# A four-layer graph network on one core: the source node numbers of all edges stay in SBUF, and the product tile of the third edge phase is held in quads

## The reference, cut to what matters

```python
sa  = ex / denom[edge_dst]                                    # layer 0: 4 heads of 16, scores q[src] * k[dst]
agg = segment_sum(sa[:, :, None] * v[edge_src], edge_dst)
h_edge = ((atom[src] + bond) @ W).reshape(-1, H, D)           # layer 1: 2 heads of 64, softmax over dst
se  = concatenate([h[src], eh]); att = sum(q * (se @ W_k))    # layer 2: 1 head of 64, softmax over dst
h   = relu(combined @ msg_w1[l] + msg_b1[l])                  # layer 3: combined = [x[src], edge features]
x   = _layernorm(x + layer(x, src, dst, ...))                 # after every layer
```

## Time and profile before

| | |
|---|---|
| median of 3 runs | 14026.2 us (14020.19 to 14042.77) |
| the profiled execution, its own time | 14023.7 us |
| its span, first to last instruction | 14022.0 us |
| PE busy | 2267.2 us (16%) |
| DVE busy | 4894.6 us (35%) |
| ACT busy | 3146.0 us (22%) |
| POOL busy | 6487.0 us (46%) |
| mean granted TensorE clock | 0.575 of full speed |
| DMA traffic | 1046.03 MB, mean 75 GB/s; 239 GB/s in the first fortieth of the span, 34 to 90 after it |

### The profile page before, as it was taken

The page is one execution under the profiler, slowest core; times in us unless marked ns, Lnnn a source line. Parts: engine busy times, 40 slices in busy tenths (PEclk is TensorE's granted clock), DMA queues, the critical chain, the costliest instruction groups (busy, mean ns, idle before and its releaser), DMA issues. The chain is left out here.

```text
span 14022.0 us, 92846 instructions
## 1 busy us (share of the span) xinstructions
PE 2267.2 (16%) x11897; PEld 1811.0 (13%) x11897; DVE 4894.6 (35%) x6191; ACT 3146.0 (22%) x3841; POOL 6487.0 (46%) x6837
## 2 busy tenths in 40 slices
PE   2000000002000000000344433444432111111112
PEld 1000000001000000000244333433330000000002
DVE  3443333345444444445222222222242222222223
ACT  0221111114111111112132222332232222222222
POOL 6644444456544444444544444444434444444444
PEclk6555555555555555555677777777765555555556
DMA  6222222221222222222222222222212222222222
GB/s 239 81 73 70 74 70 74 70 90 34 63 66 65 65 70 68 65 65 81 61 79 78 71 77 80 79 79 71 77 44 68 70 67 72 72 72 72 71 71 69
DMA packets 418910, 1046.03 MB, mean 75 GB/s; under 512 B 198760, under 2 KB 226218, under 8 KB 403804
## 3 DMA queue, kind: packets, MB, share of 16 engines
q1 hardware_dynamic: 177424, 680.51, 13.0%
q0 software_dynamic: 219488, 334.23, 10.0%
q10 hardware_dynamic: 21612, 27.96, 0.6%
HBM read 633.14 MB, written 401.95 MB: 74 GB/s over the span
## 5 line engine op out<-in xcount | busy, mean ns | idle before, releaser
L982 POOL DMA_INDIRECT se<-x_table,edge_ix x1481 | 1400.8, 946 | 1855.7 <-DMA edge_ix<-in_src 815.7
L982 POOL DMA_INDIRECT hidden<-hidden_table,edge_ix x1468 | 1388.7, 946 | 1761.0 <-DMA edge_ix<-in_src 1289.8
L982 POOL DMA_INDIRECT g<-x_table,edge_ix x1468 | 1388.5, 946 | 1648.8 <-DMA edge_ix<-in_src 1169.1
L982 POOL DMA_INDIRECT qv<-qv_table,edge_ix x1443 | 1378.6, 955 | 1404.4 <-DMA edge_ix<-in_src 865.8
L1144 ACT ACTIVATE edge_sums<-edge_val 128x1904 f32<-128x1904 f32 (+3 forms) x220 | 1116.4, 5075 | 1084.9 <-issue 1050.9
L1837 DVE TENSOR_TENSOR edge_product<-mk_ps,edge_q_now 128x256 f32<-128x256 f32 x391 | 166.1, 425 | 2308.8 <-ACT edge_msg L1772 2262.0
L1134 DVE TENSOR_TENSOR_SCAN edge_val<-edge_bank,edge_val 128x464 f32<-128x464 f32 (+1 forms) x715 | 687.6, 1032 | 672.0 <-ACT edge_val L1940 441.6
L1932 PE MATMUL edge_e_ps<-w_nodes,edge_ea_t 128*128 128x512 f32 x784 | 476.6, 774 | 2733.9 <-DMA edge_ea_t<-in_edge_attr 1165.2
L1982 DVE TENSOR_TENSOR hidden<-hidden,edge_e_ps 128x3584 f32<-128x3584 f32 x55 | 213.8, 3888 | 1799.2 <-DMA hidden<-edge_sync_rows 1232.4
L1727 PE MATMUL mk_ps<-w_mk,edge_se_t 128*128 128x128 f32 x3128 | 523.1, 320 | 1656.6 <-issue 1399.5
L1087 ACT ACTIVATE edge_bank<-edge_weight_arg 128x112 f32<-128x112 f32 (+2 forms) x171 | 38.9, 228 | 2939.9 <-issue 1980.9
(11 more groups left out here) (463 smaller groups left out, 8657.6 us busy)
## 6 DMA issues: line engine op xcount, KB each, us to landing
edge_sync_rows<-x_table SPq DMA_DIRECT2D x6656, 0.2 KB
sums<-edge_sums SPq DMA_DIRECT2D x55, 1848.0 KB
sums<-edge_sums SPq DMA_DIRECT2D x55, 1792.0 KB
sums<-edge_sums SPq DMA_DIRECT2D x55, 1008.0 KB
edge_sync_rows<-hidden_table SPq DMA_DIRECT2D x3328, 0.5 KB
sums<-edge_sums SPq DMA_DIRECT2D x55, 924.0 KB
edge_k<-k_edges SPq DMA_DIRECT2D x56, 896.0 KB
edge_bond<-in_edge_attr SPq DMA_DIRECT2D x56, 896.0 KB
```

The lines of the kernel that those rows point to most:

```text
L982: e.indirect_dma_start(self.gather_into(u, j), None, self.gather_from, bass.IndirectOffsetOnAxis(ap=now[:, j:j + 1], axis=0))\
```

## The change

`first_src` of 84 columns becomes `src` of all 1568 columns, loaded once at L385 and kept. `ix{b}`, their semaphores and the load of each chunk's numbers go, and with them the waits that stood ahead of that load on SP: the 7 parts and, for b = 1, `other_in`. POOL no longer waits for numbers. In their place POOL waits for `placed` before it gathers column J - 1 itself, and for `laid` before it gathers column J - 2 itself, from the second round on. In edge phase 2 `product` is held as two tiles of one quad that are used in turn, in place of one tile of 28 columns; the instructions are the same.

```diff
--- before.py
+++ after.py
@@ -123,7 +123,7 @@
 
         self.end_index = keep("end_index", [P, self.nodes_pp + 2 * G], U32)
         self.start_ix = keep("start_ix", [P, self.nodes_pp], U32)
-        self.first_src = keep("first_src", [P, 3 * J], U32)
+        self.src = keep("src_now", [P, self.edges_pp], U32)
         self.live = keep("live", [P, self.nodes_pp])
         self.real = keep("real", [P, self.nodes_pp])
         self.degree = keep("degree", [P, self.nodes_pp])
@@ -382,7 +382,7 @@
             load = lambda e, to, of: load_weight(p, e, to, of)
             for c in range(8, 24):
                 clear_chunk(p, e, c)
-            load(e, p.first_src[:, :], ins["src"][:, 0:3 * J])
+            load(e, p.src[:, :], ins["src"][:, :])
             e.dma_start(aside[:, :], ins["src_aside"]).then_inc(s_aside, 16)
             load(e, p.gate_bias[:, :], ins["L0_gnn_bg"].partition_broadcast(P))
             load(e, p.slope[:, :], ins["L0_gnn_prelu_a"].partition_broadcast(P))
@@ -439,7 +439,7 @@
             e.wait_ge(p.loaded, p.loads)
             for n in range(p.begun):
                 e.indirect_dma_start(p.qv_tiles[n // J][:, n % J, :], None, p.qv_table,
-                                     bass.IndirectOffsetOnAxis(ap=p.first_src[:, n:n + 1], axis=0))\
+                                     bass.IndirectOffsetOnAxis(ap=p.src[:, n:n + 1], axis=0))\
                     .then_inc(p.qv_gathered[n // J][n % J // QUAD], 16)
             e.indirect_dma_start(firsts[:, :], None, p.k_table,
                                  bass.IndirectOffsetOnAxis(ap=p.first_index[:, 0:1], axis=0)).then_inc(p.k_first, 16)
@@ -713,8 +713,6 @@
 
         self.val = [self.sb(f"val{b}", [P, self.summed_rows, J + 1]) for b in (0, 1)]
         self.sums = [self.sb(f"sums{b}", [P, J, self.width]) for b in (0, 1)]
-        self.index = [self.sb(f"ix{b}", [P, J], U32) for b in (0, 1)]
-        self.index_in = [self.sem(f"index_in{b}") for b in (0, 1)]
         self.attr_in = [self.sem(f"attr_in{b}") for b in (0, 1)]
         self.parts = parts
         self.begun = gathered is not None
@@ -783,9 +781,6 @@
         p = self.p
         out = p.sums[self.k].rearrange("(p j) f -> p j f", p=P)
 
-        def load_index(b, now):
-            e.dma_start(self.index[b][:, :], p.ins["src"][:, now]).then_inc(self.index_in[b], 16)
-
         def load(b, n):
             for tiles, of in attrs:
                 e.dma_start(tiles[b], of[:, bass.ds(n * size, size), :]).then_inc(self.attr_in[b], 16)
@@ -801,13 +796,8 @@
             if helped:
                 self.place(e, i, helps_next)
             for b in (0, 1):
-                for c in range(self.parts):
-                    self.wait_part(e, i, b, c, placed=False)
                 if b and self.sync_helps and not helped:
                     self.tell_last(e, i + 1)
-                if b and others is not None:
-                    hold(e, self.other_in, others, self.passed)
-                load_index(b, bass.ds(i * (2 * J) + (2 + b) * J, J))
                 hold(e, self.attr_free[b], at(i, 1, 1), self.passed)
                 load(b, i * 2 + (2 + b))
                 if helps_next:
@@ -963,9 +953,8 @@
             for b in (0, 1):
                 n = 2 * i + b
                 u = self.buffer(i, b)[0]
-                now = self.index[b][:, :] if n >= len(self.gathered) else self.p.first_src[:, n * J:(n + 1) * J]
+                now = self.p.src[:, n * J:(n + 1) * J]
                 if n >= len(self.gathered):
-                    e.wait_ge(self.index_in[b], 16 * i)
                     if self.begun and n in (3, 4):
                         e.wait_ge(self.rows_free[1 - b], 2)
                     else:
@@ -977,6 +966,10 @@
                     other_alone = aside and self.scalar_step > 0 and j == J - 2
                     if J * n + j < done or (last_alone and self.by_sync(i)) or (other_alone and self.by_scalar(i)):
                         continue
+                    if last_alone and i:
+                        e.wait_ge(self.placed, 16 * i)
+                    if other_alone and i:
+                        e.wait_ge(self.laid, 16 * i)
                     landed = self.last_in if last_alone else self.other_in if other_alone else \
                         self.gathered[u][j * self.parts // J]
                     e.indirect_dma_start(self.gather_into(u, j), None, self.gather_from,
@@ -991,7 +984,7 @@
             return ((0, (0, 0, 1)), (1, (0, 0, 1)), (2, (0, 0, 1)), (0, (0, 0, 2)))[2 * i + b]
         return 1 - b, (i, 1, b)
 
-    def wait_part(self, e, i, b, c, placed=True):
+    def wait_part(self, e, i, b, c):
         u, (times, per, more) = self.buffer(i, b)
         columns = 16 * J // self.parts
         if isinstance(i, int) and (i, b) == (self.rounds - 1, 1):
@@ -1008,15 +1001,10 @@
         elif isinstance(i, int) and i < 2:
             e.wait_ge(self.gathered[u][c], (columns, columns - off, columns, 2 * columns - off)[2 * i + b])
         else:
-            more = columns if b else -off
-            if placed:
-                e.wait_ge(self.gathered[u][c], at(i, columns - off * b, more))
-            else:
-                hold(e, self.gathered[u][c - 1], at(i, columns, columns * b), self.passed)
-                hold(e, self.gathered[u][c], at(i, columns - off * b, more), self.passed)
-        if b and placed and self.sync_helps:
+            e.wait_ge(self.gathered[u][c], at(i, columns - off * b, columns if b else -off))
+        if b and self.sync_helps:
             e.wait_ge(self.placed, at(i, 16, 16))
-        if b and placed and self.scalar_step:
+        if b and self.scalar_step:
             e.wait_ge(self.laid, at(i, 16, 16))
 
     def wait_gathered(self, e, i, b):
@@ -1657,7 +1645,7 @@
         q_t = [ph.sb(f"q_t{u}", [P, QUAD, P]) for u in (0, 1)]
         q_now = [ph.sb(f"q_now{u}", [P, QUAD, FD]) for u in (0, 1)]
         msg = ph.sb("msg", [P, J, FD])
-        product = ph.sb("product", [P, J, FD])
+        product = [ph.sb(f"product{u}", [P, QUAD, FD]) for u in (0, 1)]
         score = ph.sb("score", [P, 1, J])
         decay = ph.in_bank(rows * (J + 1)).rearrange("p (h f j) -> p h f j", h=1, f=rows)
         qo_ps = ctx.enter_context(nc.psum_tensor("qo_ps", [P, 2, P], F32))
@@ -1834,11 +1822,11 @@
                 u = n % 2
                 e.wait_ge(taken, at(i, per, n + 3))
                 now = slice(QUAD * c, QUAD * (c + 1))
-                e.tensor_tensor(product[:, now, :], mk_ps[u][:, :, FD:], q_now[u][:, :, :], ALU.mult)
+                e.tensor_tensor(product[u][:, :, :], mk_ps[u][:, :, FD:], q_now[u][:, :, :], ALU.mult)
                 e.scalar_tensor_tensor(msg[:, now, :], mk_ps[u][:, :, 0:FD], 0.01, msg[:, now, :],
                                        ALU.mult, ALU.max).then_inc(scored, 1)
                 e.drain()
-                e.tensor_reduce(score[:, 0, now], product[:, now, :], AX.X, ALU.add)
+                e.tensor_reduce(score[:, 0, now], product[u][:, :, :], AX.X, ALU.add)
 
             def chunk(i, b):
                 for c in range(quads):
```

## The result

The changed kernel took 14217.85 us (median of 4 runs, 14200.94 to 14227.19) against 14026.1 before (14020.19 to 14042.77): a ratio of 1.0133, with an interval of 1.0116 to 1.0151. It is slower by 1.3%, where 13,865 was forecast. The profiled execution took 14218.02 us, its span is 14216.3.

What follows compares the result with a forecast made beforehand. SP's instruction stream was taken to bound phases 0, 1 and 3. Phases 0, 1, 3, 2 and ends with openings: -134 + 65 - 44 - 53 + 5 = -161 from 14023.7, plus 2.5: 13,865 us; range 13,520 to 14,240.

Steps and rivals of the forecast that it cites:

- What bounds the kernel: SP's stream of instructions bounds phases 0, 1 and 3; DVE, ACT and POOL wait for its column.
- Step (1): SP, per chunk: load of numbers and eight satisfied waits go, 0.85 us (0.37 to 1.16), 1.7 us a round.
- The free time of 9.8 us: SP beside POOL's gathers: an unbroken run leaves SP's rows at usual speed for 9.8 us, then slows them.
- step (2): SP's middle block falls into the slow stretch: saves 3.9 us a round in phase 0, 1.4 in phase 1.
- Step (3): POOL's two runs of gathers merge in phase 1, +5.6 us a round; not in phase 0, 0.
- Phase 3: SP's block could not be placed there; removed instructions alone counted, -1.7 x 26 = -44 us.
- Step (4): Phase 2: numbers came last in one chunk of two, 2.05 us from load to gather; -53 us.
- Step (5): Ends of phases -45 us, openings of phases 1 and 3 +25 each; together +5, bounds -77 and +117.
- Step (6): Wider tile of numbers, larger prologue load, POOL's new waits and the quads cost nothing; uncovered, the load costs 3 to 10 us.
- A: Runs merge in phases 0, 1 and 3, SP's block stays in the fast part: +248 us, 14,274; chance 0.17.
- B: The place of POOL's runs does not matter, only what is removed: -227 us, 13,799; chance 0.17.
- D: Nothing changes: `rows_free` replaces the numbers at once and SP is waited for as before; 14,026 us, chance 0.09.

Runs made afterwards that it cites:

- held kernel: Changed kernel, but POOL's runs wait for SP's signal at the old load's place, behind the same waits; 13703.68 us where rows crawl, 8792.76 where nothing does.
- the free run of b = 1: Changed kernel with POOL waiting for SP's signal only for b = 0, so b = 1 starts freely; 8791.97 us where nothing crawls, crawl not reached.
- the pauses: Changed kernel, but POOL waits after columns 8, 16 and 24 until those rows landed; 12073.04 us where rows crawl, 10156.38 where nothing does.

## Why the prediction was wrong, point by point

**What bounds the kernel:** right where it was read. SP's rows bound phases 0, 1 and 3; without them the time fell by 18.9%. It was one of two states of the same kernel, which no view of one profile could show.

**Step (1), SP's instructions removed, -1.7 us a round:** not seen. In the rounds of phase 0 shown above the blocks are 16.8 us before and 16.8 after, and over the phase 14.2 and 14.7. The held kernel, which lacks only the load, has blocks 0.2 to 0.4 us shorter in phases 0, 1 and 3.

**The free time of 9.8 us, and step (2) with it:** this is the step that failed. The prediction read from one run in phase 1 that every run leaves SP alone for 9.8 us, wherever it starts, and moved this number to runs that start in the midst of SP's rows. From it, step (2) had 64 rows done at 25.8 us after the copy and the crawl at 27.4 in phase 0, so that the block fell into the crawl, -3.9 us a round. Measured: the rows start 4.2 or 4.9 us after the copy in most rounds (3.6 forecast) and need 23.2 without a crawl (22.2 forecast), so they would be done at 27.4 to 28.1, and the crawl begins at 24.0 to 24.7: 16.9 or 17.6 until the run's start, and 7.1 more in the median. The first 64 rows got out ahead of it in none of the 23 rounds, and the block came after it. That alone would only lose the saving. What goes with the loss is the shorter free time of both runs: a round has 28.4 crawling rows in place of 24.1, its rows take 6.9 us more and its blocks 0.5, and the period grows by 7.4 us where -5.6 was forecast. The number could have been doubted beforehand, since the trace of the kernel before has medians of 9.7, 8.4 and 7.5 us in the three phases. In phase 1 the block did fall into the crawl, and that saved nothing: the blocks grew by 6.0 us, the rows fell by 3.6, as many rows crawled as before, and the round came out 2.3 us longer.

**Step (3), merging:** wrong in phase 1. There the runs were forecast to meet and stayed some 6 or 12 us apart in all rounds but one; the phase still lost 57 us (65 forecast), so the agreement there is by chance. Where they were made to meet, it cost 10.4 to 13.4 us a round over the held kernel and 3.2 to 11.5 over the one before, against 5.6.

**Phase 3**, taken at -44 with the block left out: +34, and 30.1 crawling rows in place of 27.9. **Step (4), phase 2:** -30 against -53. The reading that the numbers were last in one chunk of two is near the trace, where their load ended POOL's wait 32 times and PE 22 times; why only some half of the time came back is not shown. **Step (5):** its openings cost what was forecast, some 25 us each: the first round between copies takes 138.1 us against 112.9 before in phase 1 and 139.5 against 118.9 in phase 3. The table of the periods counts them in those phases, and the second round of phase 0, 138.5 against 113.7, is a third that was not forecast. All else came out at -39, near the -45 taken for the ends, but in part elsewhere: the stretch between the copies of phase 0 and phase 1 fell from 596.5 to 572.9 us, that behind phase 3's last copy from 323.8 to 312.1. **Step (6):** the wide tile, the load in the prologue and POOL's new waits cost nothing that can be told: the first copy in phase 0 is at 654.0 against 651.4, and at 647.0 in the held kernel, and the changed kernel ties where nothing crawls. The quads cost nothing there either.

**The rivals:** A had the sign and nearly the size (14,274), but not the mechanism; the runs did not meet. B, that the place of the runs does not matter, is refuted by the held kernel. The Trainium skill ("DMA: Bandwidth & Descriptors", "Issuing engines are not separate DMA queues") says that the sequencer's time to initiate a DMA is usually small beside the DMA itself. These rows are a case in which it is not: without them the kernel is 18.9% faster where rows crawl. Where nothing crawls, 64 rows still take 23 us of issue, and they are hidden. D's tie is what came out wherever nothing crawled, but for another reason: POOL gathers without a pause there, and neither numbers nor free rows nor SP are waited for.

**Open:** what makes the crawl begin later in the held kernel, which beats the one before by 2.3% (the load gone from SP, or POOL's start at SP's signal, without the load's way to SBUF), and whether the free run of b = 1 does harm of its own; both kernels that would tell ran only where nothing crawls. What makes the surroundings was not found either.

## What to carry to other kernels

A wait that looks like pure loss on one engine (4140.4 us of idle POOL) can hold two engines in step, and when it goes, what moves is the overlap of the others: ask what runs beside what, before the wait and after it. A duration read at one place (9.8 us of free time, from one run) is not a constant: read it in every phase, and ask whether the change moves what it depends on. If the trigger is needed and the transfer is not, keep the trigger: the held kernel also keeps the numbers in SBUF, and it was not slower than before in either surroundings. And time a change in more than one session: here the same pair of kernels gave +1.3% and a tie, and the pauses -14% and +16%.

## What the runs showed of the hardware

In one of the two surroundings, SP's sequencer falls beside an unbroken run of gathers to one instruction in up to 1.4 us: a move and a transfer of 0.70 us each, and a row every 2.8 us at worst. How long it is free at first goes with where the run starts. In the first fetches of phase 1 a run that starts 5.6 us ahead of SP's rows (held) leaves 12.3 us, one that starts 1.8 ahead (before) 9.1, and one that starts 17.2 us into them (changed) 6.0, all medians; in phase 0 it is 9.9 at 3.4 ahead, 9.0 at 1.7 ahead and 7.1 at 12.7 into them. The second fetches do not fall into this order so plainly: before, it is 11.2 at 0.6 ahead in phase 0 and 7.2 at 0.2 ahead in phase 1. The first ones would fit a store of instructions that rows use up faster than blocks do, and two rows of the profile for ACT in the changed kernel suggest the same. ACT starts to fetch 10 us into a run, when SP has been crawling for some 3 us (2182 to 2184.3 us, then 2184.5 to 2208):

```profile
L861 ACTq DMA_DIRECT2D edge_scalar_rows<-qv_table x6: 222/223/456, 2182.2 to 2184.0; - x6
...
L861 ACTq DMA_DIRECT2D edge_scalar_rows<-qv_table x10: 23/694/738, 2184.7 to 2207.9; - x10
```

Its first six rows go at the usual pace and the next ones at SP's, as if some 13 instructions (seven moves and six transfers) had been in store and the rest came slowly. DVE shows nothing of it in the same stretch: seven of its instructions start within 1.7 us, 2188.54 to 2190.21. POOL itself slows down in the kernel without rows, in the same surroundings, where its runs are a whole phase long:

```profile
999.55 1.09 POOL L975 DMA_INDIRECT qv<-qv_table,src_now  x1 [0.30 <-issue]
1000.95 1.09 POOL L975 DMA_INDIRECT qv<-qv_table,src_now  x1 [0.31 <-issue]
1002.35 1.09 POOL L975 DMA_INDIRECT qv<-qv_table,src_now  x1 [0.30 <-issue]
```

A gather comes every 1.40 us there, against 1.25 in short runs; where nothing crawls the changed kernel gathers without a pause, too, and a gather takes 944 ns, not 1090. The Trainium skill ("Runtime: NRT & Kernel Launch", "Instruction fetch mechanics") says that the sequencer streams its instructions by itself and that the cost of going from one block of them to the next is mostly hidden; the rows above would not be explained by that. A supply that is slowed by the gathers is argued here and was not tested. One thing in the traces speaks against its simplest form: the 376 packets, most of them of 8 KB, in which the changed kernel's instructions arrive take 380 ns in the median where rows crawl, and 380 where nothing does.
